# A two-layer mixture-of-experts kernel: sorted rows stored as two 16-bit parts and loaded by transposing DMAs, norms in pairs of fused steps, experts chosen from logits

## The reference

```
h      = relu(x W1[lang] + b1[lang])                 # 32 wide
x2     = LN(x + h W2[lang] + b2[lang]) * gamma[lang] + beta[lang]
xn     = LN(x2) * gamma + beta
probs  = softmax(xn gate_w);  w, idx = top_k(probs, 2);  w = w / sum(w)
out    = x + x2 + sum over the two chosen experts of w_e (gelu(xn w1_e + b1_e) w2_e + b2_e)
```

## Time and profile before

| | |
|---|---|
| median of three runs | 386.85 us (386.45 to 387.94) |
| the profiled execution's own time | 388.65 us |
| its span, first to last instruction | 386.8 us |
| mean granted TensorE clock | 0.965 |
| busy PE / DVE / ACT / POOL | 91% / 68% / 66% / 59% |
| DMA | 40.94 MB, mean 106 GB/s |

### The profile page before, as it was taken

The page is one execution under the profiler, slowest core; times in us unless marked ns, Lnnn a source line. Parts: engine busy times, 40 slices in busy tenths (PEclk is TensorE's granted clock), DMA queues, the critical chain, the costliest instruction groups (busy, mean ns, idle before and its releaser), DMA issues.

```text
span 386.8 us, 7491 instructions
## 1 busy us (share of the span) xinstructions
PE 353.4 (91%) x2092; PEld 203.7 (53%) x2093; DVE 263.0 (68%) x760; ACT 256.2 (66%) x451; POOL 226.6 (59%) x211
## 2 busy tenths in 40 slices
PE   8997999999999999969879786979999899999982
PEld 6765554444444454544445342437978787444430
DVE  0467748877649986757977757317798985367661
ACT  2465477877867657948794472649889898756650
POOL 6499999100026888717555786733378460287884
PEclk9999999999999999989998896969999999999998
DMA  7749922620066763642540111121324225631221
GB/s 204 256 104 371 399 89 67 179 43 0 9 169 140 144 128 72 151 93 70 100 120 17 58 43 35 47 71 44 109 76 128 67 69 90 157 94 42 66 57 54
DMA packets 47456, 40.94 MB, mean 106 GB/s; under 512 B 6978, under 2 KB 41522, under 8 KB 47290
## 3 DMA queue, kind: packets, MB, share of 16 engines
q1 hardware_dynamic: 44632, 36.12, 34.7%
q0 software_dynamic: 1760, 3.71, 3.3%
q10 hardware_dynamic: 1026, 0.65, 0.5%
HBM read 28.80 MB, written 11.67 MB: 105 GB/s over the span
## 4 chain that ended last, share of the span: by engine, by line
PE 57%; DVE 13%; POOL 12%; issue 11%; DMA 2%; ACT 2%; POOLq 0%; SPq 0%; DVEq 0%; ACTq 0%
PE bank L640 12%; POOL whl L1820 6%; PE bank L589 6%; PE bank L591 6%; PE bank L590 6%; PE bank L651 3%; PE bank L652 3%; PE bank L653 3%; POOL acc L767 3%; DVE l L699 2%; PE bank L566 2%; PE bank L1037 1%; PE bank L1341 1%; PE bank L1090 1%; PE bank L568 1%
## 5 line engine op out<-in xcount | busy, mean ns | idle before, releaser
L675 ACT ACTIVATE h<-bank,b1f 128x512 f32<-128x512 f32 x160 | 105.2, 686 | 84.1 <-PE bank L640 61.3
L699 DVE SCALAR_TENSOR_TENSOR l<-h 128x512 f16<-128x512 f32 x118 | 93.3, 794 | 20.7 <-ACT h L687 16.0
L767 POOL TENSOR_TENSOR acc<-acc,tmp 128x512 f32<-128x512 f32 x47 | 69.9, 1487 | 62.4 <-DVE tmp L740 60.0
L640 PE MATMUL bank<-h,w 128*128 128x512 f32 x160 | 83.3, 603 | 0.0
L687 ACT ACTIVATE h<-h 128x512 f16<-128x512 f32 x108 | 67.9, 629 | 2.1
L589 PE MATMUL bank<-xh,whl 128*128 128x512 f16 x128 | 49.3, 385 | 0.0
L591 PE MATMUL bank<-xh,whl 128*128 128x512 f16 x128 | 49.2, 385 | 0.0
L590 PE MATMUL bank<-xl,whl 128*128 128x512 f16 x128 | 49.2, 385 | 0.0
L1820 POOL DMA_INDIRECT whl<-sorted_out,idx x24 | 24.1, 1006 | 24.6 <-DMA sorted_out<-yo 18.3
L640 PEld LDWEIGHTS bank<-h,w 128*128 128x128 f32 x160 | 30.7, 195 | 11.6 <-issue 0.6
L669 ACT ACTIVATE h<-bank,b1f 128x256 f32<-128x256 f32 x76 | 31.4, 474 | 4.8 <-PE bank L568 2.6
(11 more groups left out here) (225 smaller groups left out, 710.1 us busy)
## 6 DMA issues: line engine op xcount, KB each, us to landing
Gs<-gates SPq DMA_DIRECT2D x40, 256.0 KB, 5.1
wraw<-in_w SPq DMA_DIRECT2D x16, 512.0 KB, 3.8
sorted_in<-zer SPq DMA_DIRECT2D x14, 448.0 KB, 6.7
wraw<-sorted_in SPq DMA_DIRECT2D x19, 128.0 KB, 2.2
sorted_out<-yo SPq DMA_DIRECT2D x19, 128.0 KB, 1.8
first<-in_xtm SPq DMA_DIRECT2D x1, 1024.0 KB, 8.9
mg<-in_gbc SPq DMA_DIRECT2D x8, 128.0 KB
w<-in_w SPq DMA_DIRECT2D x8, 128.0 KB, 2.8
```

What stands on the lines that cost most here:

```text
L640: pe.matmul(o[:, :], w2[:, e, j * 128:j * 128 + 128], h32[:, u % NH, :], start=(c == 0), stop=(c == 3))\
L675: act.activation(h32[:, u % NH, :], bank[u % 4][:, :], ACT.Gelu if layer else ACT.Gelu_apprx_tanh, bias=b1f[layer][:, e * 4 + c:e * 4 + c ...
L699: dve.scalar_tensor_tensor(l16[:, slot(u), :], h32[:, u % NH, :], HS, h16[:, slot(u), :], ALU.mult, ALU.subtract).then_inc(s_lo, 1)
L767: pool.tensor_tensor(a, a, tmp[:, i % NTMP, :], ALU.add).then_inc(s_acc, 1)
```

## The change

- `sorted_in` holds, in 512 bytes per row, a high and a low float16 part of the row (`xs`) in place of a float32 row. The values stored are those after gamma and beta, scaled by 16 (`XS`); `fgr` is gamma and beta of the second norm, spread over all partitions. Per group ScalarE writes the high parts (`act_rows`) and GpSimd the low ones (`pool_rows`).
- A tile's input is loaded by two transposing DMAs from SP, one for each part (256 rows by 128 columns), straight into `xt`, from where `pe_m1` reads. The TensorE transposes, the ScalarE pass, the VectorE cast and the GpSimd subtraction of a tile go, and so do the banks that the transposes took. The load of tile i waits for the second unit of tile i-3.
- Each norm is two fused VectorE steps: (x - mean) * gamma, which doesn't need the root, and (...) * root + beta. They take the place of `n1`, the multiply, the add and `n2`.
- The choice of experts (`choice`) is made from logits. The weights (`weights`) come later, from exp(second - first) as a pow with base e on GpSimd. `pe_rank` waits for `m_oh`, the end of the choice. ScalarE has no exp in the middle part.
- All groups get new places (`MID`, `LATE`). `w2`'s loads have a semaphore each. The argument of `add` has another name; it is queued on GpSimd in both kernels.

```diff
-PLACE = [
-    {"lg": 17.6, "d": 17.2, "exp": 17.4, "top": 17.8, "rank": 24.5, "scatter": 9.7},
-    {"h": 2.0, "act_h": 2.2, "lg": 17.6, "d": 17.2, "exp": 17.4, "top": 17.8, "rank": 22.5, "scatter": 2.9},
-    {"h": 1.7, "act_h": 2.0, "xa": 3.0, "stats": 3.1, "rstd": 3.6, "n1": 4.6, "stats2": 6.2, "rstd2": 6.0, "n2": 8.3,
-     "x2T": 11.3, "x2a": 11.8, "nT": 10.3, "xn": 10.5, "lg": 12.2, "d": 11.8, "exp": 12.3, "top": 13.4, "rank": 15.8,
-     "scatter": 2.0},
-    {},
-]
+MID = {
+    "h": 1.6, "act_h": 1.5, "xa": 3.1, "stats": 3.6, "rstd": 4.4, "s1": 4.6, "s2": 5.6, "stats2": 6.7, "rstd2": 7.6,
+    "n2a": 7.8, "n2": 8.9, "nT": 10.9, "xn": 10.4, "hi": 10.5, "lo": 11.0, "lg": 12.3, "d": 11.5, "top": 11.7,
+    "rank": 13.55, "e": 13.5, "w": 16.6, "x2T": 12.9, "x2a": 13.2, "cT": 20.5, "scatter": 2.0,
+}
+LATE = {
+    "h": 1.5, "act_h": 1.5, "xa": 3.3, "stats": 3.6, "rstd": 4.4, "s1": 5.5, "s2": 7.0, "stats2": 8.5, "rstd2": 9.4,
+    "n2a": 9.8, "n2": 11.2, "nT": 13.5, "xn": 12.9, "hi": 13.1, "lo": 13.6, "lg": 15.3, "d": 14.5, "top": 14.7,
+    "rank": 17.2, "e": 16.4, "w": 20.6, "x2T": 16.9, "x2a": 17.2, "cT": 24.5, "scatter": 2.0,
+}
+PLACE = [LATE, MID, MID, {"s1": 5.5, "s2": 7.5, "n2a": 10.2, "lg": 17.6, "d": 17.2, "top": 17.8, "e": 19.0, "w": 21.5}]
...
-        scx = nc.dram_tensor("sorted_in", [E * CAP + TS, D], F32, kind="Internal").ap()
+        scx = nc.dram_tensor("sorted_in", [E * CAP + TS, 2 * D], F16, kind="Internal").ap()
+        xs = sb("xs", [128, TA, 2 * D], F16)
+        xt = sb("xt", [128, NX, 2 * TS], F16)
...
                     if c == 0:
-                        pe.wait_ge(t_xl, v + 1)
+                        pe.wait_ge(t_xr[v % NX], 32 * (v // NX + 1))
...
+            def dve_s1(dve):
...
+                    last = dve.scalar_tensor_tensor(n1[:, i * 128:i * 128 + 128], o[:, i * 128:i * 128 + 128], mv[:, 0, i, 0:1],
+                                                    gbc[:, 2 * g + i // 2, 0:D], ALU.subtract, ALU.mult)
...
+            def dve_s2(dve):
...
+                    last = dve.scalar_tensor_tensor(x2[:, i * 128:i * 128 + 128], n1[:, i * 128:i * 128 + 128], rs[:, 0, i:i + 1],
+                                                    gbc[:, 2 * g + i // 2, D:2 * D], ALU.mult, ALU.add)
...
+            def act_rows(act):
+                act.wait_ge(m_n2, g + 1)
+                act.activation(rows_of(0), n2f[:, :].rearrange("p (t d) -> p t d", t=4), ACT.Copy).then_inc(m_xh, 1)
+
+            def pool_rows(pool):
+                pool.wait_ge(m_xh, g + 1)
+                pool.tensor_tensor(rows_of(1), n2f[:, :].rearrange("p (t d) -> p t d", t=4), rows_of(0), ALU.subtract)\
+                    .then_inc(m_xs, 1)
...
+            def pool_e(pool):
+                pool.wait_ge(m_dd, g + 1)
...
+                pool.tensor_tensor(ee[:, :], base[:, :], dd[:, :], ALU.pow).then_inc(m_e, 1)
...
-                pe.wait_ge(m_cw, g + 1)
+                pe.wait_ge(m_oh, g + 1)
...
-                    sp.wait_ge(s_w, E)
-                    sp.wait_ge(s_w16, E)
                 if i >= NX:
-                    sp.wait_ge(t_tr, i - NX + 1)
+                    sp.wait_ge(s_m1, US + 2 * (i - NX) + 2)
                 r = sp.value_load(tei[0:1, 2, i:i + 1], min_val=0, max_val=E * CAP)
-                sp.dma_start(xr[:, i % NX, :, :], scx[bass.ds(r, TS), :].rearrange("(z p) d -> p z d", p=128))\
-                    .then_inc(t_xr[i % NX], 16)
+                for k in range(2):
+                    sp.dma_start(xt[:, i % NX, k * TS:k * TS + TS], scx[bass.ds(r, TS), k * D:k * D + D], transpose=True)\
+                        .then_inc(t_xr[i % NX], 16)
...
-            at("sp", p - 1 if i < NX else tpos(i - NX) + 0.5, sp_in)
-            at("pe", mpos[("t", i)], pe_t)
-            at("act", p + 0.1, act_x)
-            at("dve", p + AT["tdve"], dve_x)
-            at("pool", p + 0.3, pool_x)
+            at("sp", p - 1 if i < NX else US + 2 * (i - NX) + 2.3, sp_in)
```

More of the change, by code:

```diff
@@ L314, in build_adaln_ffn @@
         s_w16 = sem("s_w16")
-        s_w2b = sem("s_w2b")
+        s_w2b = [sem(f"s_w2b{e}") for e in range(E)]
         s_w2f = sem("s_w2f")
@@ L512, in tpos @@
             return max(US - 0.4 + 0.05 * i, US + 2 * i - 5 + AT["tile"])
-        for i in range(NTL):
-            misc.append((tpos(i), ("t", i), (t_x32, i + 1)))
         for g in range(GA):
@@ L1479, in _ @@
                     else:
[L1480 to L1492 removed]
+                        dve.wait_ge(m_cw, g)
                     for i in range(4):
[L1494 removed]
+                        last = dve.max(mx8[:, i, :], lg[:, i, :])
                     return last
@@ L1527, in _, with weights, part @@
                         def _(dve, i=i):
-                            return dve.tensor_tensor(cumb[:, i + 1, :], cumb[:, i, :], OB[:, i, :], ALU.add)
+                            ins = dve.tensor_tensor(cumb[:, i + 1, :], cumb[:, i, :], OB[:, i, :], ALU.add)
+                            if i == 4 * g + 3:
+                                ins.then_inc(m_oh, 1)
+                            return ins
+                return parts
+            def weights():
+                parts = []
+                def part(fn):
+                    parts.append(fn)
                 @part
                 def _(dve):
+                    dve.wait_ge(m_oh, g + 1)
+                    dve.wait_ge(m_e, g + 1)
+                    return dve.tensor_scalar(c4[:, :, 0], ee[:, :], 1.0, None, ALU.add)
+                @part
+                def _(dve):
+                    return dve.reciprocal(wk[:, :, 0], c4[:, :, 0])
+                @part
+                def _(dve):
+                    return dve.tensor_tensor(wk[:, :, 1], ee[:, :], wk[:, :, 0], ALU.mult)
+                @part
+                def _(dve):
+                    if g:
+                        dve.wait_ge(m_cT, g)
+                    if g < GA:
+                        dve.tensor_copy(wA[:, sl, :], wk[:, :, :])
                     for k in range(2):
@@ L1581, in mid @@
             at("pe", mpos[("lg", g)], pe_lg)
-            at("dve", m + after("d", g), dve_d)
-            at("act", m + after("exp", g), act_exp)
-            spread("dve", "dve", m + after("top", g), 0.15, top())
+            at("dve", m + after("d", g), dve_lg)
+            spread("dve", "dve", m + after("top", g), 0.15, choice())
+            at("pool", m + after("e", g), pool_e)
+            spread("dve", "dve", m + after("w", g), 0.15, weights())
             at("pe", mpos[("cT", g)], pe_cT)
```

197 lines of the change are left out of this document (79 added, 118 removed).

## The result

| | before | after |
|---|---|---|
| median | 386.65 us (386.04 to 387.94, 4 runs) | 396.31 us (395.45 to 398.51, 4 runs) |
| span of the profiled execution | 386.8 us | 393.8 us |
| mean granted TensorE clock | 0.965 | 0.975 |
| first tile matmul | 255.48 us | 251.02 us |
| last tile's first matmuls | 322.97 us | 329.8 us |

The ratio of after to before is 1.0254, with a 95% interval of 1.0204 to 1.0304: the change is slower. So they are compared by their ratios to before; 0.01 of ratio is 3.9 us, and the interval of a ratio is in brackets behind it.

A forecast was written before the change was run, and what follows sets the result against it. TensorE was taken as the bound, losing about 24 us to waits and lower clock from 158 to 262 us. Gains 7 + 5 + 5 + 0 + 5.9 = 22.9, less 1, gave median 365 us, own range 355 to 375, overall 354 to 388.

The forecast's parts named there:

- Part five: Tile stage: without the tile's transposes, casts and other passes, 5.9 us gained, bounds 3 and 9, if the DMAs keep up.
- 0.9 + 3.5 is inside 5.3: Tile stage: register read 0.9 us plus transposing pair 3.5 fit the two-tile lead of 5.3 us.
- Rival (a): Tile stage: non-overlapping transposing DMAs, 5.1 us per pair, set the pace; slower, about 399 us; chance 0.15.
- Part three: Start of the tiles: earlier rank and shorter input path cut TensorE's wait; 5 us gained, bounds 1 and 7.
- x = 3.5: Start of the tiles: us taken for the transposing load before the first tile matmul, from a range of 2.2 to 5.1.
- Part one: Middle part: without exp's table loads on ScalarE, both TensorE waits for hTs go; 7 us gained, bounds 4 to 8.5.
- Part two: Middle part: choosing experts from logits shortens the chain before the rank matmul; 5 us gained, bounds 2 and 7.
- Part four: Normalisation: fused VectorE steps replace scalings and GpSimd passes; term 0, bounds -4 and +3 us over four groups.
- the 1 us of overlap: Whole kernel: 1 us taken off the summed gains because gains at neighbouring handovers overlap.

The follow-up runs named there:

- one_transpose: Kernel after the change, with each tile's input in one transposing DMA of 512 rows instead of two of 256: 376.95 us, ratio 0.9729.
- sp_relief: Kernel after the change, with the stores of yo and the w2 loads issued by GpSimd instead of SyncE: 382.94 us, ratio 0.9857.
- exp_back: one_transpose with the exponential taken by ScalarE again instead of as a power on GpSimd: 380.76 us, ratio 0.9839.
- exp_only: Kernel before the change, with only the exponential of all 32 logits moved to GpSimd as a power, at the old place: 402.33 us, ratio 1.0362.
- later_places: one_transpose with everything from the transposes of n2 on 2 places later in group 0 and 3 in group 1: 374.28 us, ratio 0.9645.
- later_rank: later_places with the rank matmuls of groups 1 and 2 put 1.8 and 0.65 places later: 372.51 us, ratio 0.9587.
- short_adds: one_transpose with each GpSimd addition cut to 32 of 512 columns, rest of the sums left out: 372.31 us, ratio 0.9614.
- plain_loads: Kernel after the change, with a tile's two transposing DMAs replaced by plain ones of the same bytes, values wrong: 377.98 us, ratio 0.9741.
- third_issue: Kernel after the change, plus one unused transposing DMA of 32 rows per tile on SyncE: 420.32 us, ratio 1.0814.
- old_tiles: Kernel after the change, with sorted rows and tile input put back to those of before: 384.93 us, ratio 0.9931.

## Why the prediction was wrong

**Part five, the tile stage, failed, and the sign with it.** The term was 5.9 us gained; 11.5 were lost. Its condition, that the DMAs keep up, was weighed with a price for the pair, 3.5 us from issue to landing, and with the number of pieces. Both concern the transfer, and the transfer was not the limit: the first pair took 3.8 us from its issue (247.24) to the first matmul, and a whole tile transposed in one DMA lands in 2.5. The step that failed is "0.9 + 3.5 is inside 5.3": it sets the time until one tile's rows are there against a lead of two tiles, and never adds up how long SyncE is busy in each round. The trace of before held the plain issue at 0.38 us, and no time of a transposing one; the experiments put it at 1.15. A pair is thus 2.3 us, 2.6 as a mean with the long ones. With the store, the eight `w2` loads, the row number (0.5; 0.9 was put on it) and the time between instructions, SyncE needs 4.5 us per round against 2.9 to 3.6 per tile before. Where SyncE has one such issue per tile (`one_transpose`) the stage takes 61.1 us, 6.5 less than before: but for this wait the term of 5.9 was near.

**Rival (a)** named this wait, tiles 4 us or more apart and the sign, and gave 399 us for a measured 396.3. Its mechanism was another: it wanted transfers that don't overlap, 5.1 us for each pair. `sp_relief`, with the same transfers, refutes that. It also counted 17 us of gains from parts one to three, of which 4.5 came. So the rival's number was near by luck.

The Trainium skill's sentence that such transposes are as fast as ordinary DMAs ("Advanced Engine Details and Errata", X-Bar Transpose (TRN2)) agrees with the landing (2.5 us for 128 KB in `one_transpose`, 2.2 for the plain load) and is silent on the issue. The 1309 ns that the Trainium skill gives for a 128x128 block ("VectorE: DVE Perf Modes", The three transpose paths) don't add up over blocks: four of them land in 2.5 us in `one_transpose`. The Trainium skill's page "Perfetto Trace Analysis", What "DMA-bound" means, lists as a bound of its own an issuing engine whose row is solid with DMA slices. The row of SyncE after the change is close to that: of the 58.2 us from 264.35 to 322.50, DMA issues fill 45, and register reads and what lies between instructions the rest.

**Part three, the start of the tiles,** left 1.2 us missing; 4.1 are. The rank matmul, VectorE's steps behind it and the first and last scatter in the kernel after:

```profile
231.31 0.18 PE L1633 MATMUL bank<-OB,triu 128*128 128x32 bf16 x1 [1.41 <-issue]
```

```profile
232.65 1.14 DVE L1654 TENSOR_TENSOR oh<-OH,rk 128x32 f32<-128x32 f32 x2
```

```profile
234.54 1.07 POOL L1753 DMA_INDIRECT sorted_in<-xs,idx  x1 [0.90 <-DVE idx L1661]
...
244.19 0.95 POOL L1753 DMA_INDIRECT sorted_in<-xs,idx  x1 [0.30 <-issue]
```

From rank to the first scatter 3.2 us pass (1.7 were put on it; the two steps of 1.14 take 0.29 in group 1, and here one of them lies beside an addition), the scatters take 10.6 (10.2), to the issue it is 2.1 (2.2), and from there to the matmul 3.8 (x = 3.5). Together that is 19.7 us, and TensorE's dense work behind the rank matmul ends near 247.0, after 15.7 us (16.4). So half of the miss is the way from rank to scatter, 1.5 us; the others are small, and together they make 2.9.

**Part one, exp leaves ScalarE.** The table loads went as said. The `hTs` waits went too, but `exp_back` has none either, and `exp_only` keeps half of them, so the new places are what removes them here. Putting the exponential back costs about 4 us, the lower bound of the term of 7, and the traced execution doesn't show where. Whether the mechanism of this part was right stays open.

**Part two, rank ahead of the weights.** The chain from the logits (226.64) to the last running count (231.21) is 4.6 us, forecast 4.4. Group 2's wait is 1.4 us, forecast 1.6, but group 1 has one of 1.4 that wasn't there before. Turning the order back costs 5.6 us, for a term of 5. So the gain was forecast well. The length of the chain was hit partly by luck: one of the four running sums is held up for 1.1 us beside an addition, which wasn't in the sum, and the other steps were quicker than was put on them. The four sums in group 0, where no addition lies beside them, and in group 2:

```profile
167.71 0.75 DVE L1530 TENSOR_TENSOR cumb<-cumb,OB 128x8 bf16<-128x8 bf16 x4
```

```profile
229.39 1.82 DVE L1530 TENSOR_TENSOR cumb<-cumb,OB 128x8 bf16<-128x8 bf16 x4
```

**Part four, normalisation, term 0.** Much of the gain of the middle part went here. TensorE's waits for the normalised rows rose from 2.1 us to 8.0, and so did the time at half clock in 158:196 (granted clock 0.91 for 0.96), while in 196:231 the clock rose from 0.90 to 0.95. The mean of a fused step was bounded well (0.58 as the upper end). What the mean hides is that single steps (three in group 0, one each in groups 1 and 2) are blocked for 0.7 to 1.7 us beside an addition of GpSimd, on the path to the transposes. Since the new places put those transposes early, the blocks add to TensorE's waits. `later_places` and `later_rank` win back 0.0142 of ratio, 5.5 us, by order alone. With short additions the waits for `n2f` are 1.5 us and the tiles start 15 us earlier (`short_adds`), though its time falls by 4.5 only.

**The sum.** Ahead of the tiles 17 us were forecast (7 + 5 + 5), less the 1 us of overlap, and 4.5 came; in the tiles 5.9 were forecast and -11.5 came. The second miss is shown by five runs (`sp_relief`, `plain_loads`, `one_transpose`, `third_issue`, `old_tiles`). Of the first, 2.9 us are those of part three, and some 5.5 us are traced to the places and the blocks. `short_adds` shows that what GpSimd's additions hold up is larger than the whole first miss. How it divides between parts one, two and three is not settled, for the parts were only turned back singly, at the places of the change.

## What to carry to other kernels

A DMA has two prices: its transfer, and the time of the engine that issues it. Add up the second per round of the loop, as one does for a compute engine, and for a new kind of DMA measure it first; where it goes by the instruction, one large DMA with a strided read behind it is the better shape. When work moves to VectorE, look whether its operands lie in SBUF or PSUM and what GpSimd reads at that moment, and put the consumer's place behind the worst case, not behind the mean.

## What the runs showed of the hardware

- A transposing DMA costs SyncE 1.15 us to issue at the median, for 256 or 512 rows, and 1.23 for 32; a plain one of the same rows 0.38. Single ones take up to 2.1 us in the kernel after.
- Four VectorE steps of 128x128 with both inputs in SBUF take 1.13 us with no full addition beside them and up to 3.15 beside GpSimd's additions; even a running sum of 128x8 goes from 0.16 to 1.2 us. A GpSimd addition takes 1.26 us undisturbed and up to 3.12 beside VectorE's passes. With one input in PSUM the VectorE step stays at 0.34 us.
- A power on GpSimd takes 1.05 us for 4 elements per partition and 5.45 for 32.
